# Perceiver layer 4: one head's maxima in 4 of 16 steps by ScalarE and GpSimd instead of VectorE

## What is computed

```
q = split_heads(query @ Wq.T + bq)       # 4 batches, 16 heads, 256 queries, 16
k = split_heads(key @ Wk.T + bk)         # 4 batches, 16 heads, 4096 keys, 16
v = split_heads(value @ Wv.T + bv)
scores = jnp.einsum('bhqd,bhkd->bhqk', q, k) / np.sqrt(HEAD_DIM)
weights = jax.nn.softmax(scores, axis=-1)
out = jnp.einsum('bhqk,bhkd->bhqd', weights, v)
return out.transpose(0, 2, 1, 3).reshape(b, -1, D_MODEL) @ Wo.T + bo
```

## Time and profile before

| | |
|---|---|
| median of 3 runs | 1947.66 us (1938.59 to 1957.48) |
| the profiled execution | 1944.65 us, of which the span of the profile is 1942.8 us |
| granted TensorE clock over the span | 0.956 of full |
| busy over the span | PE 1761.3 us (91%), DVE 1450.4 us (75%), ACT 1171.6 us (60%), POOL 369.7 us (19%) |
| layer 4's maxima | from 1066.3 to 1749.9 us |

### The profile page before, as it was taken

The page is one execution under the profiler, slowest core; times in us unless marked ns, Lnnn a source line. Parts: engine busy times, 40 slices in busy tenths (PEclk is TensorE's granted clock), DMA queues, the critical chain, the costliest instruction groups (busy, mean ns, idle before and its releaser), DMA issues. The chain is left out here.

```text
span 1942.8 us, 32676 instructions
## 1 busy us (share of the span) xinstructions
PE 1761.3 (91%) x12516; PEld 1209.4 (62%) x12516; DVE 1450.4 (75%) x1677; ACT 1171.6 (60%) x2109; POOL 369.7 (19%) x244
## 2 busy tenths in 40 slices
PE   6999998989989984999988799999999999999855
PEld 5877777457757763887867455555555555555524
DVE  6547553577899864656563799999999999997575
ACT  0333332577777734435342288888888988887373
POOL 4133210144445511222212000010000000000000
PEclk8999999999999996999999899999999999999887
DMA  9798871158957833112134956557466655530000
GB/s 359 262 338 321 292 271 37 63 179 289 322 212 274 310 133 103 60 55 82 58 60 74 174 108 118 95 115 134 94 114 118 111 103 112 114 66 15 1 0 22
DMA packets 171815, 280.05 MB, mean 144 GB/s; under 512 B 21598, under 2 KB 100478, under 8 KB 164494
## 3 DMA queue, kind: packets, MB, share of 16 engines
q1 hardware_dynamic: 169934, 277.48, 50.7%
q10 hardware_dynamic: 1728, 0.49, 0.2%
HBM read 187.33 MB, written 88.14 MB: 142 GB/s over the span
## 5 line engine op out<-in xcount | busy, mean ns | idle before, releaser
L2332 DVE TENSOR_REDUCE xn_peaks<-psum 128x2 f32<-128x1024 f32 x512 | 621.8, 1224 | 47.6 <-PE psum L2130 39.5
L2287 ACT ACTIVATE moe_mix_transposed<-psum 128x512 f32<-128x512 f32 x1024 | 552.6, 597 | 70.1 <-PE psum L2135 38.3
L2135 PE MATMUL psum<-xn_q_stack,xn_k_words 50*128 50x256 f32 x2048 | 376.5, 306 | 14.5 <-ACT y_normed L2257 7.8
L2135 PEld LDWEIGHTS psum<-xn_q_stack,xn_k_words 50*128 50x128 f32 x2048 | 249.3, 186 | 215.0 <-ACT moe_mix_transposed L2287 184.7
L2130 PE MATMUL psum<-xn_k_words,xn_q_stack 50*128 50x512 f32 x1024 | 372.8, 451 | 6.1 <-DMA xn_q_stack<-q_rows 4.0
L2167 PE MATMUL psum<-moe_mix_transposed,xn_v 128*32 128x256 f32 x4096 | 327.8, 392 | 2.0 <-issue 0.3
L2130 PEld LDWEIGHTS psum<-xn_k_words,xn_q_stack 50*128 50x128 f32 x1024 | 185.5, 185 | 14.2 <-DVE xn_peaks L2332 7.8
L933 POOL TENSOR_TENSOR mx_state<-mx_du,mx_b_all_channels 128x1024 f32<-128x1024 f32 x64 | 154.0, 2407 | 198.0 <-ACT mx_b_all_channels L1110 85.9
L1191 DVE TENSOR_TENSOR_SCAN mx_state<-psum,mx_state 128x1024 f32<-128x1024 f32 x64 | 146.2, 2284 | 49.3 <-ACT psum L1120 41.9
L324 PE MATMUL psum<-xw_ctx_natural,xw_weights_transposed 128*128 128x256 f32 x512 | 125.6, 391 | 12.5 <-DVE xw_weights_transposed L476 12.3
L2167 PEld LDWEIGHTS psum<-moe_mix_transposed,xn_v 128*32 128x32 f32 x4096 | 81.7, 108 | 73.9 <-issue 7.7
(11 more groups left out here) (348 smaller groups left out, 2556.8 us busy)
## 6 DMA issues: line engine op xcount, KB each, us to landing
xn_k_words<-k_words SPq DMA_DIRECT2D x384, 128.0 KB, 6.6
ctx_words<-xw_ctx_transposed_words SPq DMA_DIRECT2D x64, 512.0 KB
ctx_chunk_words<-ctx_words SPq DMA_DIRECT2D x64, 512.0 KB, 5.5
k_words<-ctx_k_words SPq DMA_DIRECT2D x128, 256.0 KB, 2.5
v_all<-ctx_v SPq DMA_DIRECT2D x32, 544.0 KB, 3.2
xn_v<-v_all SPq DMA_DIRECT2D x32, 544.0 KB, 4.9
xw_mask<-in_mask_BxSxS_ik SPq DMA_DIRECT2D x8, 2048.0 KB, 8.0
xw_ctx_natural<-in_ctx SPq DMA_DIRECT2D x32, 512.0 KB, 6.8
```

Of the source, the lines that this page charges most:

```text
L2135: return pe.matmul(PS[:, narrow_bank("exp", n, step, a), half * S:(half + 1) * S], K[n % XN_KSLOTS][narrow_rows(a), kt * P:(kt + 1) * P], ...
L2287: act.activation(t["weights"][:, step % 4, a, :, :], bank.rearrange("p (t s) -> p t s", t=2), ACT.Exp, scale=XN_SCALE).then_inc(s.taken, 1)
L2332: dve.tensor_reduce(t["peaks"][:, m % 2, q, :, c], PS[:, 2 * (x % 2):2 * (x % 2) + 2, :], AX.X, ALU.max).then_inc(s.top_read, 1)
```

## The change

From pair 4 on, four of the 16 indices of a pair are *side* indices: i = 0, 3, 6, 9 (112 in all, 28 pairs by 4). There

- VectorE reduces only head 0's bank (128 x 512 instead of 128 x 1024);
- ScalarE copies head 1's bank, 128 x 512, to SBUF between its two exponentials of that step (`side`); two buffers take turns, so a copy also waits until GpSimd has finished with the buffer (`larger`, two sides back);
- GpSimd halves those 512 scores three times, to 256, 128 and 64 maxima (`larger`). Each halving is three instructions, max(low, high) being written as high + max(low - high, 0): a subtraction of two tensors, a clamp with two constants, an addition of two tensors. Each waits for the one before it;
- at the pair's end VectorE reduces the 4 x 64 maxima in two more small reductions before its `shift`, and `shift` first waits until GpSimd has finished all four sides of the pair.

TensorE, before it writes x, also waits for the copy of x - 2. The DMAs are the same.

```diff
+XN_SIDE_FROM, XN_SIDE_STEPS, XN_SIDES, XN_SIDE_END = 4, (0, 3, 6, 9), 2, 64
+XN_SIDE_OPS = 3 * (BANK // XN_SIDE_END).bit_length() - 3
+XN_HUGE = 3.0e38
...
+    def larger(x):
+
+        i, m, c, q = XN_SIDE_OF[x], x // XN_TOP, x % XN_TOP // QT, x % QT
+        at, width = i * XN_SIDE_OPS, BANK // 2
+        pool.wait_ge(s.side, i + 1)
+        if m >= XN_SIDE_FROM + 2:
+            pool.wait_ge(s.side_read, QT * (m - 1 - XN_SIDE_FROM))
+        if at:
+            pool.wait_ge(s.larger, at)
+        z = t["side"][:, i % XN_SIDES, :]
+        while width >= XN_SIDE_END:
+            low, high, gap = z[:, 0:width], z[:, width:2 * width], t["gap"][:, 0:width]
+            pool.tensor_tensor(gap, low, high, ALU.subtract).then_inc(s.larger, 1)
+            pool.wait_ge(s.larger, at + 1)
+            pool.tensor_scalar(gap, gap, XN_HUGE, 0.0, ALU.min, ALU.max).then_inc(s.larger, 1)
+            pool.wait_ge(s.larger, at + 2)
+            z = high if width > XN_SIDE_END else t["sides"][:, m % 2, q, XN_SIDE_STEPS.index(x % XN_TOP) // QT, :]
+            pool.tensor_tensor(z, high, gap, ALU.add).then_inc(s.larger, 1)
+            at += 3
+            if width > XN_SIDE_END:
+                pool.wait_ge(s.larger, at)
+            width //= 2
...
     for n in range(XN_N):
+        for i in XN_SIDE_STEPS if XN_SIDE_FROM <= n + 1 < XN_N else ():
+            larger(XN_TOP * (n + 1) + i)
...
             pool.wait_ge(s.words, 2 * (n + 1))
+            if n + 1 >= XN_SIDE_FROM:
+                pool.wait_ge(s.larger, XN_SIDE_OPS * narrow_sides_upto(n + 1))
...
+        if x - 2 in XN_SIDE_OF:
+            pe.wait_ge(s.side, XN_SIDE_OF[x - 2] + 1)
...
+    def side(x):
+
+        i = XN_SIDE_OF[x]
+        act.wait_ge(s.top, 2 * x + 1)
+        if i >= XN_SIDES:
+            act.wait_ge(s.larger, XN_SIDE_OPS * (i - XN_SIDES + 1))
+        act.copy(t["side"][:, i % XN_SIDES, :], PS[:, 2 * (x % 2) + 1, :]).then_inc(s.side, 1)
...
-            for a in range(2):
-                exponentials(n, step, a)
+            exponentials(n, step, 0)
+            if XN_STEPS * n + step + XN_TOP + XN_LEAD in XN_SIDE_OF:
+                side(XN_STEPS * n + step + XN_TOP + XN_LEAD)
+            exponentials(n, step, 1)
...
+        if narrow_side(x):
+            dve.tensor_reduce(t["peaks"][:, m % 2, q, 0, c:c + 1], PS[:, 2 * (x % 2), :], AX.X, ALU.max
+                              ).then_inc(s.top_read, 1)
+            return
...
     def shift(m):
+        if m >= XN_SIDE_FROM:
+            dve.wait_ge(s.larger, XN_SIDE_OPS * narrow_sides_upto(m))
+            for q in range(QT):
+                chunks = [i // QT for i in XN_SIDE_STEPS if i % QT == q]
+                dve.tensor_reduce(t["peaks"][:, m % 2, q, 1, chunks[0]:chunks[1] + 1:chunks[1] - chunks[0]],
+                                  t["sides"][:, m % 2, q, :, :], AX.X, ALU.max).then_inc(s.side_read, 1)
+            dve.wait_ge(s.side_read, QT * (m + 1 - XN_SIDE_FROM))
```

More of the change, by code:

```diff
@@ L1752, with narrow_side, narrow_sides_upto @@
 XN_LATE = 24 * S
+XN_SIDE_FROM, XN_SIDE_STEPS, XN_SIDES, XN_SIDE_END = 4, (0, 3, 6, 9), 2, 64
+XN_SIDE_OPS = 3 * (BANK // XN_SIDE_END).bit_length() - 3
+XN_HUGE = 3.0e38
+def narrow_side(x):
+    return x // XN_TOP >= XN_SIDE_FROM and x % XN_TOP in XN_SIDE_STEPS
+XN_SIDE_OF = {x: i for i, x in enumerate(filter(narrow_side, range(XN_N * XN_TOP)))}
+def narrow_sides_upto(m):
+    return len(XN_SIDE_STEPS) * max(m + 1 - XN_SIDE_FROM, 0)
 def narrow_mix_bank(i):
@@ L1804, in narrow_tiles @@
          "choice": sb("choice", [P, 2, 2, XN_DH]), "ident": sb("identity_words", [P, P], F32R), "den": sb("denominators", [P, 2, S // XN_SPREAD]), "rsum": k.Y[:, 0:KD, :]}
+    t["side"] = k.Y[:, KD:KD + 4, :].rearrange("p (i t) d -> p i (t d)", i=XN_SIDES)
+    t["gap"] = k.Y[:, KD + 4, :]
+    t["sides"] = k.YT[:, 0, 0:2 * BANK].rearrange("p (i q j n) -> p i q j n", i=2, q=QT, n=XN_SIDE_END)[:, :, :, 0:2, :]
     late = k.moe_mixT[:].rearrange("p e s -> p (e s)")
@@ L1818, in narrow_sems @@
                      "neg words sum acc o_in den_in r_out r_in halves den ident o wide row plus x "
-                     "choice chosen last_den last_o last_pe")
+                     "choice chosen last_den last_o last_pe side larger side_read")
     return s, [k.xn_keys_in] + [k.sem_row(f"xn_keys{slot}_", XN_KHALVES) for slot in range(1, XN_KSLOTS)], k.sem_row("xn_values", 2)
```

## The result

| | before | changed kernel |
|---|---|---|
| median (lowest to highest, executions) | 1943.68 us (1938.59 to 1957.48, 4) | 1969.87 us (1966.71 to 1974.27, 4) |
| the profiled execution | 1944.65 us | 1974.27 us, span 1972.4 us |
| granted TensorE clock over the span | 0.956 | 0.947 |
| maxima of pair 3 to pair 31 (28 pairs) | 586.7 us | 1782.0 - 1161.9 = 620.1 us |

The ratio is 1.0125, 95% interval 1.0065 to 1.0185: slower by 26 us by the medians, where 81 had been forecast (2026 us, 1988 to 2100). The direction is right; the size is off by a factor of three and outside the range. (The kernel before has one execution more here than in its table ahead, so its median is 1943.68 and not 1947.66.) The profiled execution is the longest of its four; the clocks of the other three are 0.951 and 0.952.

What follows compares the result with a forecast made beforehand. GpSimd's closed loop was to bound the pair at 23.35 us: 28 turns make 653.8, plus 14.3 of other GpSimd work 668.1 in place of 586.7, so +81.4 on 1944.65 gives 2026 us, range 1988 to 2100.

Steps and rivals of the forecast that it cites:

- TensorE bounds, and VectorE's relief is worth nothing: Layer 4 maxima before the change: TensorE has no gap, so less VectorE work wins at most a few tenths per batch.
- Rival C: VectorE paced the loop and GpSimd's side is under 4.74 us: a pair loses 1.6 us, 1900 us; chance 0.03.
- The clamps' price: GpSimd's three clamps in a side, priced from tensor-by-scalar rows with one operation: 1.88 us.
- rival B: Clamps run at a cast's pace, a side 4.54 us, GpSimd hidden, ScalarE nearly full: 1950 us, no change; chance 0.09.
- The closed loop: GpSimd's four sides of 5.5 us plus 1.35 us until the next pair's first side: no pair under 23.35 us.
- the threshold of 4.74: Time per side in us from which GpSimd binds, as four sides and 1.35 us then exceed the pair's 20.3.
- 1.35 us of turn-round: From the fourth side's end through VectorE's reductions and GpSimd's words to the next pair's first side.
- ScalarE's copies at no cost: Four copies, 2.3 us a pair beside 18.2 us of ScalarE work, cost nothing in a pair of 23 us.
- the cover: The pair lengthened to 23 us by GpSimd's loop, within which ScalarE's copies were to cost nothing.
- VectorE saves 0.53 us at a side index and pays 0.49 back: VectorE's reduction falls from 1.22 to 0.69 us; two extra reductions at the pair's end cost 0.49; all idle time.
- The clock: If TensorE's granted clock, 1.00 before, fell in the new gaps, steps would grow and the sum be too low.
- A: The main case: GpSimd binds at about 5.5 us a side, giving 2026 us; chance 0.80.

Runs made afterwards that it cites:

- spread: Changed kernel with side indices 0, 5, 8, 11 in place of 0, 3, 6, 9, and two halvings a side in place of three; 1953.82 us, ratio 1.0040.
- no_copies: Changed kernel without ScalarE's copies: GpSimd halves old data once VectorE has read the index, VectorE reduces both heads in full; 1966.35 us, ratio 1.0107.
- column_clamp: Changed kernel with each clamp a single maximum against a column of zeros, in place of minimum and maximum against two constants; 2084.69 us, ratio 1.0719.
- copies_spread: Kernel before plus only ScalarE's four copies a pair, at indices 0, 5, 8, 11; no GpSimd halvings, VectorE's reductions whole; 1944.33 us, ratio 1.0003.

## Why the prediction was right or wrong

**TensorE bounds, and VectorE's relief is worth nothing: right.** VectorE's time in a pair fell by 1.65 us and no plain pair got shorter, not even with the long steps taken away (spread). Rival C falls with that.

**The clamps' price: wrong, and it decided.** The failing term is "no row has a clamp with two constants ... I take 1.88". It measured 0.95. The chosen rows were true for their own form; that the form with two constants could be quicker than any with one was in neither bound. "I see nothing in the rows that makes a GpSimd instruction of these sizes faster" closed the range from below, though rival B, three paragraphs on, had just such a price (0.92) from the casts. The sentence of the Trainium skill beside it (GPSIMD Engine Reference, Engine selection: work with one input is roughly at line rate) agrees with this form's 405 ns, a cast's pace (396), and not with the 848 to 1071 ns of the other three.

**The closed loop: right in its working.** With the clamps' true price the same sum gives 3.05 + 0.95 + 9 x 0.09 = 4.81 us a side, as measured, and a turn of 20.3 us, which is the pair's length to a tenth. The side is 0.07 us above the threshold of 4.74, but that was made with 1.35 us of turn-round: with the 1.24 measured, and without the 0.17 that the side's 4.81 already has, it is 4.81 too (no_copies). GpSimd stands just at the edge of binding. column_clamp confirms the same sum at the other price: 24.4 worked out, 24.5 measured.

**ScalarE's copies at no cost: wrong, and this is where most of the 26 us come from.** The prediction did say "were the cover gone (a pair of 20.3), ScalarE would be full", and priced a late ScalarE at 0.05 us by the earlier trace rows. Cover and price failed together. The 0.15 us that it read as ScalarE's spare time is the idle time that the row gives ahead of four exponentials, by their spans; from start to start two of them take 0.97 us of a step of 1.235. The earlier trace rows is a step with the casts alone ahead of it; the copy comes on top of them, one step after another, and then ScalarE has 0.2 us of copy and 0.74 us of casts to make up. Rival B got the mechanism and allowed 112 copies 0 to 0.1 us each; they cost 0.69 / 4 = 0.17 on average, in truth nothing at steps 3 and 10, 0.46 at step 13 (in two step distances) and 0.23 at step 0. A sum per copy can't show that; its place among ScalarE's other work does. Over 28 pairs that is 19 us of the 26. The other 7 have the size of the difference between spread and copies_spread, but no run shows that they are the same.

**The direction: luck.** A slowdown was forecast because GpSimd would bind. GpSimd did not, and the slowdown came from the term put at nothing.

**VectorE saves 0.53 us at a side index and pays 0.49 back: right** (0.69 us instead of 1.23, and 0.47 for the two reductions).

**The clock: named, not counted.** The last paragraph said that a fall would make the sum too low. In the changed kernel's profile the pairs with a fall carry 12.4 us of the 33.4. In column_clamp the stage is some 26 us above what had been expected, and its eight pairs beside a fall that take 27 to 30 us hold some 30 us above 24.5 each, so falls probably carry most of it. Had the clamp's price been right, 2026 would have been too low for this reason.

**The chances.** 0.80 for A rested on one interpolated price; B had 0.09. The outcome is B's kernel (GpSimd hidden, ScalarE nearly full) at 1970 in place of 1950.

## What to carry to other kernels

The price of an instruction form that no row shows has to be bounded from the cheapest form of that engine as well, above all where the forecast turns on a threshold: here 0.95 against 1.88 us decided whether 22 or 19 us stood against a pair of 20.3. Before work is put on an engine that is 90% busy "in the gaps", go through its stream step by step: here it cost nothing where a quiet step followed, and 0.2 to 0.5 us just ahead of that engine's own extra work. Taking work from an engine that nobody waited for bought nothing.

## What the runs showed of the hardware that I had not expected

- GpSimd's tensor-by-scalar with minimum and maximum against two constants takes 402, 295 and 242 ns for 128 x 256, 128 and 64; with one constant 848, 526 and 366; with a column 921, 601 and 441; with multiply and maximum 1071, 640 and 427.
- Where VectorE's additions of two SBUF tiles and GpSimd's halvings met, the one that began second took longer. This addition of 128 x 512 began 0.02 us after a two-tensor instruction of GpSimd and took 1.26 us; the clamp of 128 x 256 that GpSimd began while it ran took 0.72 in place of 0.40:

```profile
1669.56 1.26 DVE L2433 TENSOR_TENSOR x_residual<-x_residual,moe_mix_transposed 128x512 f32<-128x512 f32 x1
```

```profile
1669.54 0.73 POOL L1986 TENSOR_TENSOR y_normed<-y_normed 128x256 f32<-128x256 f32 x1
1670.36 0.72 POOL L1988 TENSOR_SCALAR y_normed<-y_normed 128x256 f32<-128x256 f32 x1
```

  Before, the three of that line took 681 ns on average. VectorE's reductions out of PSUM kept their 1.23 us beside the same work. Whether this is where the 7 us between spread and copies_spread come from is not shown.
- In column_clamp TensorE ran at half clock for 7 to 24 us in fourteen places, twelve of them during or right after a step of 3.2 to 5.1 us in an otherwise full stream; two steps of 3.19 and 3.25 us had no fall behind them. In the window shown, 13.7 us at half clock hold steps of 2.16 in place of 1.24 us. By that ratio the same work would take 7.9 us at full clock: an estimated 5.8 us more, which is above the 3.28 us of the stall itself. (Part of it is hidden there, as GpSimd sets that kernel's pair.)
